# Layer-norm scaling of layers one and two moved from VectorE to ScalarE, with an offset computed on GpSimd, in a four-layer graph network kernel

## The reference

```python
x = _layernorm(x + L0(x, nodemask, adj, adj, ...))   # attention, 8 heads, mixed with adj and exp(-adj)
x = _layernorm(x + L1(x, adj, W))                    # relu([x, adj@x/deg] @ W.T)
x = _layernorm(x + L2(x, adj, ...))                  # two hypergraph convolutions, relu and layer norm between
x = _layernorm(x + L3(x, adj, ...))                  # gated attention over adj

def _layernorm(x, axis=-1, eps=1e-05):
    m = jnp.mean(x, axis=axis, keepdims=True)
    v = jnp.var(x, axis=axis, keepdims=True)
    return (x - m) / jnp.sqrt(v + eps)
```

## Time and profile before

| what | value |
|---|---|
| median of 3 runs | 1185.15 us |
| the profiled execution | 1184.85 us, span 1182.8 us |
| mean granted TensorE clock | 0.986 of full |
| PE busy | 1127.0 us (95%) |
| DVE busy | 919.8 us (78%) |
| ACT busy | 595.7 us (50%) |
| POOL busy | 572.5 us (48%) |

### The profile page before, as it was taken

How to read it: one execution, slowest core, us unless ns; L and a number is a source line. 1 busy time by engine, 2 the same in 40 slices (tenths; PEclk the granted TensorE clock), 3 DMA queues, 4 the chain that set the end, 5 groups by cost and what they waited for, 6 DMA issues and landing times.

```text
span 1182.8 us, 29171 instructions
## 1 busy us (share of the span) xinstructions
PE 1127.0 (95%) x10416; PEld 951.4 (80%) x10416; DVE 919.8 (78%) x2223; ACT 595.7 (50%) x1266; POOL 572.5 (48%) x731
## 2 busy tenths in 40 slices
PE   5889999999999999999999999999999999999875
PEld 4768888888888888888888888888888888888763
DVE  6675887878788887878877788788778878777865
ACT  2536465454646445474544647454464645546331
POOL 2426356382644628264472735537273553826341
PEclk9899999999999999999999999999999999999897
DMA  7010102010010201001020100102001010100000
GB/s 233 24 28 1 46 3 67 1 48 21 22 44 0 67 0 44 22 22 44 0 67 0 43 24 22 44 0 67 0 23 44 18 49 0 42 8 28 2 23 18
DMA packets 52868, 37.22 MB, mean 31 GB/s; under 512 B 28182, under 2 KB 47707, under 8 KB 52827
## 3 DMA queue, kind: packets, MB, share of 16 engines
q1 hardware_dynamic: 51272, 35.09, 9.7%
q10 hardware_dynamic: 1554, 1.58, 0.5%
HBM read 28.27 MB, written 8.39 MB: 31 GB/s over the span
## 4 chain that ended last, share of the span: by engine, by line
PE 90%; DVE 5%; ACT 2%; POOL 1%; issue 1%; DMA 0%; SPq 0%; POOLq 0%; DVEq 0%; ACTq 0%
PE bank L1022 22%; PE bank L1024 21%; PE bank L1023 20%; PE bank L1093 3%; PE bank L1128 3%; PE bank L1163 2%; PE bank L1220 2%; PE bank L1201 2%; PE bank L1106 2%; PE bank L1294 2%; PE bank L1258 2%; DVE oT_lo L709 2%; PE bank L1083 1%; PE bank L1284 1%; PE bank L1248 1%; PE bank L1182 1%
## 5 line engine op out<-in xcount | busy, mean ns | idle before, releaser
L529 POOL TENSOR_TENSOR prob<-prob,srec 128x512 f32<-128x512 f32 x64 | 71.6, 1118 | 146.9 <-DVE srec L832 146.9
L467 POOL TENSOR_SCALAR var<-mv 128x2 f32<-128x2 f32 x128 | 29.0, 227 | 208.6 <-DVE mv L779 208.6
L786 DVE TENSOR_SCALAR x<-x,mv,rstd 128x256 f32<-128x256 f32 x256 | 119.0, 522 | 3.8 <-POOL rstd L470 3.3
L590 ACT ACTIVATE v<-bank 64x256 f32<-64x256 f32 x256 | 96.7, 378 | 17.7 <-PE bank L1024 15.4
L477 POOL TENSOR_TENSOR bhT<-hT,be 128x512 f32<-128x512 f32 x16 | 18.3, 1144 | 168.3 <-PE bank L1172 168.3
L775 DVE BATCH_NORM_STATS2 stats<-x 128x6 f32<-128x256 f32 x256 | 96.4, 418 | 4.4
L470 POOL TENSOR_TENSOR rstd<-var,negh 128x2 f32<-128x2 f32 x128 | 91.1, 712 | 10.7
L534 POOL TENSOR_TENSOR prob<-prob,mix 128x512 f32<-128x512 f32 x64 | 86.7, 1355 | 6.0 <-POOL prob L529 1.9
L918 DVE TENSOR_TENSOR hT_lo<-r,hT_hi 128x512 fp32r<-128x512 f32 x64 | 69.7, 1089 | 22.4 <-ACT hT_hi L633 22.2
L1022 PE MATMUL bank<-wo_hi,oT_hi 128*128 128x256 f32 x256 | 75.1, 293 | 8.9 <-DVE oT_lo L709 8.9
L1022 PE MATMUL bank<-w_hi,hT_hi 128*128 128x258 f32 x256 | 75.8, 296 | 2.7 <-DVE hT_lo L918 2.1
(11 more groups left out here) (202 smaller groups left out, 3697.9 us busy)
## 6 DMA issues: line engine op xcount, KB each, us to landing
xTin<-in_x_t SPq DMA_DIRECT2D x32, 256.0 KB, 2.8
xin<-in_x SPq DMA_DIRECT2D x16, 512.0 KB, 3.7
out_x<-x SPq DMA_DIRECT2D x32, 256.0 KB
adjA<-in_adj SPq DMA_DIRECT2D x16, 128.0 KB, 2.5
adjB<-in_adj_t SPq DMA_DIRECT2D x32, 64.0 KB, 3.1
adjC<-in_adj_t SPq DMA_DIRECT2D x32, 64.0 KB, 2.3
r<-in_wqkv ACTq DMA_DIRECT2D x2, 512.0 KB, 4.1
x<-in_wqkv SPq DMA_DIRECT2D x1, 512.0 KB, 8.2
```

What stands on the lines that cost most here:

```text
L529: pool.tensor_tensor(rows_of(u), rows_of(u), srec[:, k, :].rearrange("p (h a) -> p h a", a=1) .broadcast_to([P, 2 * HP, N]), ALU.mult).the ...
L590: ins = act.activation(v[e * N:(e + 1) * N, i, gr, :, :], src[gr * N:(gr + 1) * N, e], ACT.Copy)
L786: ins = dve.tensor_scalar(x[:, t, :], x[:, t, :], mv[layer][:, t, 0:1], rstd[layer][:, t:t + 1], ALU.subtract, ALU.mult)
```

## The change

The steps `scale0` and `scale1` go from VectorE's order to ScalarE's. ScalarE computes x * rstd + offset with one activation (Identity, per-partition scale and bias) for each tile. GpSimd makes the offset: after `rstd` it multiplies the mean by `rstd` in place and multiplies that by -1 into `var`, with a wait on its own semaphore before each. Layers 2 and 3 keep VectorE's `scale`.

```diff
+SHIFTED = (0, 1)
 ACT_ORDER = [
 ...
-    ("A", "v", 0), ("D", "y3", 3), ("B", "graph_d", 0), ("A", "shift", 1), ("A", "v", 1), ("B", "spread", 0),
+    ("D", "y3", 2), ("A", "v", 0), ("D", "y3", 3), ("B", "graph_d", 0), ("A", "shift", 1), ("A", "v", 1),
+    ("B", "scale1", 0), ("B", "spread", 0), ("B", "spread", 1), ("A", "v", 2), ("B", "up", 0), ("B", "hid_hi", 0),
 ...
-    ("N", "k", 0), ("N", "q", 0), ("N", "q", 1), ("B", "hyper", 0), ("N", "q", 2), ("B", "hyper", 1), ("N", "q", 3),
+    ("A", "pv", 2), ("A", "pv", 3), ("N", "k", 0), ("N", "q", 0), ("N", "q", 1), ("B", "hyper", 0),
+    ("A", "scale0", 0), ("N", "q", 2), ("B", "hyper", 1), ("N", "q", 3), ("A", "scale0", 1),
 ]
@@ inv_root, on GpSimd
                 pool.tensor_tensor(rstd[layer][:, lo:hi], var[layer][:, lo:hi], negh[:, lo:hi],
                                    ALU.pow).then_inc(SEM[f"rstd{n}"], 1)
+                if layer in SHIFTED:
+                    pool.wait_ge(*count(f"rstd{n}", g, k + 1))
+                    apart(pool, g)
+                    pool.tensor_tensor(mv[layer][:, lo:hi, 0], mv[layer][:, lo:hi, 0], rstd[layer][:, lo:hi],
+                                       ALU.mult).then_inc(SEM[f"mean_rstd{n}"], 1)
+                    pool.wait_ge(*count(f"mean_rstd{n}", g, k + 1))
+                    apart(pool, g)
+                    pool.tensor_scalar(var[layer][:, lo:hi], mv[layer][:, lo:hi, 0], -1.0, None,
+                                       ALU.mult).then_inc(SEM[f"offset{n}"], 1)
@@ on ScalarE
+            def scale(g, layer, x, lo, hi, ready, k):
+
+                act.wait_ge(*count(f"offset{layer}", g, k + 1))
+                for t in range(lo, hi):
+                    ins = act.activation(x[:, t, :], x[:, t, :], ACT.Identity, bias=var[layer][:, t:t + 1],
+                                         scale=rstd[layer][:, t:t + 1])
+                ins.then_inc(SEM[ready], 1)
 ...
+                "scale0": lambda g, i: scale(g, 0, xl[0], 2 * i, 2 * i + 2, "x1_ready", i),
+                "scale1": lambda g, i: [scale(g, 1, xl[1], 2 * k, 2 * k + 2, "x2_ready", k) for k in range(2)],
@@ on VectorE
             def scale0(g, i):
-                scale(g, 0, xl[0], 2 * i, 2 * i + 2, "x1_ready", i)
                 if isinstance(g, int) and g == 0 and i == 1:
                     other_weights(3)
 ...
-                "scale1": lambda g, i: [scale(g, 1, xl[1], 2 * k, 2 * k + 2, "x2_ready", k) for k in range(2)],
```

More of the change, by code:

```diff
@@ L116 @@
 PER = {
-    "xT_in": 32, "x_in": 16, "adjA_in": 16, "adjB_in": 32, "adjC_in": 32, "mask_in": 16, "out_done": 32, "xT_hi": 2, "xT_lo": 2, "mask_rows": 2,
+    "xT_in": 32, "x_in": 16, "mean_rstd0": 2, "offset0": 2, "mean_rstd1": 2, "offset1": 2, "adjA_in": 16, "adjB_in": 32, "adjC_in": 32, "mask_in": 16, "out_done": 32, "xT_hi": 2, "xT_lo": 2, "mask_rows": 2,
     "xb_ready": 1, "expA_ready": 1, "mix_sum": 1, "mix_ready": 1,
```

## The result

The changed kernel takes 1251.05 us (median of 4 runs, 1250.60 to 1252.28) against 1185.01 us before: a ratio of 1.056, 95% interval 1.054 to 1.058. It is slower, as forecast, but by 66 us where 43 were forecast, and 1251.05 lies above the range of 1212 to 1246. The profiled span is 1249.6 us against 1182.8.

The account below looks back on a forecast made before the run. TensorE was taken as the bound, busy 69.35 of 69.79 us a round. The terms 35 + 3.5 + 0.8 + 6.3 + 0.9 - 3.1 = 43.4 us on 1184.85 gave 1228 us, range 1212 to 1246.

Parts of the forecast that it names:

- `spread`, 14 groups: Groups 1 to 14: layer 1's scalings queue behind `v 1`, making TensorE's tile 2 2.5 us late: 35 us (30 to 36).
- `spread`, group 0: Group 0, where ScalarE is behind with `v 1`: the last layer 1 scaling ends 3.5 us late.
- `spread`, group 15: Group 15, which has no `v`: scalings 1.35 us late, of which a later wait takes back some 0.5: 0.8 us.
- `turn1`, 14 groups: End of the round: layer 0's second scaling pair makes `turn1`'s tile 2 0.45 us late: 6.3 us (1.5 to 8.5).
- group 15's open chain: Group 15, where PE waits 3.56 us for the scaling: GpSimd's two operations and ScalarE's pair add 0.9 us.
- `mask` of group 0: Group 0: PE's 3.3 us wait for `mask` falls to 1.4 and the clock stays up: gain 3.1 us (1.9 to 3.6).
- The upper ends: ScalarE's price: the second per-partition operand costs as much as the first, 0.59 us a scaling, 0.49 from start to start.
- Identity needed no other table: Rival on ScalarE: Identity isn't in the loaded table, costing 5.1 us in each of 15 rounds: 1305 us; chance 0.02.
- Hidden, as forecast: GpSimd's added 2.8 us a round fits beside 34 us of idle time, with nothing on the path.
- the clock falls in every round: Rival: behind `spread`'s pause TensorE runs at 1.2 GHz, 16 times, adding 19 to 27 us: 1247 to 1255; chance 0.13.
- in a few rounds only: Milder form of the clock rival: some rounds lose the clock, adding 2 to 8 us, which the range holds.
- the two tiles inside the pause: Argument against the clock rival: `spread`'s 2.4 us pause is in two pieces, with two tiles of work inside.

Follow-up runs that it names:

- E: The changed kernel with layer 1's scaling moved earlier in ScalarE's order, behind `y3 0` instead of `v 1`: 1188.97 us, ratio 1.004.
- F: The changed kernel with 7 unread 128x512 products before tile 0 of `spread` (14 in group 0, none in group 15): 1233.66 us, ratio 1.041.
- the split one: The changed kernel with layer 0's scaling back on VectorE, only layer 1's on ScalarE: 1237.34 us, ratio 1.045.

## Why the forecast was wrong, step by step

The account of the 66.8 us between the spans, from differences of periods: before, changed, the kernel with layer 1 early (E, whose full rounds are 70.32 us, its first 61.51 and its 15th 64.34), and the one with `spread` filled (F: 73.03, 64.87 and 67.03).

| step | forecast | measured | from |
|---|---|---|---|
| `spread`, 14 groups | 35 | 37.9 | 14 x (73.03 - 70.32) |
| `spread`, group 0 | 3.5 | 3.4 | first period, F - E |
| `spread`, group 15 | 0.8 | 0.6 | `turn1`'s x6 row to `up`: 28.38 - 27.77 |
| `turn1`, 14 groups | 6.3 | 7.4 | 14 x (70.32 - 69.79) |
| group 15's open chain | 0.9 | 0.9 | 64.34 - 62.52 - 0.53 = 1.3, less 0.4 inside `turn1` |
| `mask` of group 0 | -3.1 | -3.1 | first period, E - before |
| sum | 43.4 | 47.1 | |
| clock, 10 rounds | 0 | 15.8 | 10 x 1.58 |
| clock, group 0 | 0 | 1.2 | first period, changed - F |
| before the first `turn1` | 0 | 1.5 | 66.78 - 65.27 |
| the last 50 us (put down to the clock, not shown) | 0 | 1.2 | 52.98 - 51.82 from `up` to the end |

Together 66.8. Every mechanism in the sum was right, and its 47.1 us alone would have stayed inside the range; two sizes were a little small (2.71 us for 2.5, 0.53 for 0.45), and with the clock up the kernel would be where the filled one is, 1233.66 us, inside the range.

*ScalarE's price.* The upper ends, 0.59 us and 0.49 from start to start, were right: 590 ns, and 2.07 us for four against 2.06. The Trainium skill (ScalarE: Activation LUTs, "What ACT_TABLE_LOAD costs") gave 0.585; the trace agrees, so the second per-partition operand costs as much as the first. Identity needed no other table.

*GpSimd.* Hidden, as forecast, and shown by the run that added only its work.

*`mask` in group 0.* The wait fell to 0.8 us and not to 1.4, because TensorE comes later out of `turn1`, where it now waits itself. From the start of `turn1` to the product that needs `mask`, TensorE takes 3.85 us in the kernel with layer 1 early against 5.73 before: 1.9 us less, as forecast. The clock stays at 1.00 behind it, which is the rest of the 3.1.

*Group 15.* The parts were priced well in sum, not in kind. Its waits, of TensorE and then of ScalarE, against the earlier trace rows:

```profile
1164.69 0.41 PE L1182 MATMUL bank<-ident,x 128*128 128x128 f32 x2 [1.14 <-ACT x L641]
1168.24 1.54 PE L1182 MATMUL bank<-ident,x 128*128 128x128 f32 x6 [3.14 <-ACT x L641]
```

```profile
1162.93 0.63 ACT L668 ACTIVATE r<-r 128x512 f32<-128x512 f32 x1 [3.63 <-POOL r L525]
1163.47 1.08 ACT L641 ACTIVATE x<-x,var,rstd 128x256 f32<-128x256 f32 x2
```

The first pair stands behind a tanh that waited 3.63 us for GpSimd. I had looked at the second pair only.

*The step that failed* is the weighing of the clock. In the sum it had no term at all. The forecast put "the clock falls in every round" at 0.13 and "in a few rounds only" at 2 to 8 us. It was neither: 10 of 13, 17.0 us. The rival's price was right (up to 1.7 us a time, 1.6 measured); its chance was not. That 1251.05 lies inside the rival's 1247 to 1255 is partly luck: it had 16 losses, on a sum that was 3.7 us too small. The argument against it leaned on one pause of 1.7 us that had kept the clock and on the two tiles inside the pause. One pause that kept it says little, since pauses of 1.98 and 0.21 us both kept it and lost it in this one kernel. The two tiles did not protect either: the pause in one piece of 2.32 us lost 5 of 13 rounds, the split one 5 of 13 in a round of nearly the same length. What those rows could carry was "some rounds, number unknown", 0 to 16 times 1.6 us, a range of 1228 to 1254 with no reason to favour its low end.

*The start.* The 1.5 us ahead of the first `turn1` aren't charged to the change: in runs where nothing ahead of it was changed it came at 65.27 to 67.89 us. In the last 50 us the kernel before runs at half clock in part too, so their 1.2 us aren't charged to the change either; one stretch of before and then one of after, each beginning 25.0 us behind the first product of `up`:

```profile
1155.98:1165.98 10.00, 8.56 (x35) 6.33 (x36) 3.59 (x8) 2.75 (x5) 0.00 (x0) 0.63 0.00 0
```

```profile
1221.62:1231.62 10.00, 8.37 (x23) 6.33 (x24) 3.36 (x7) 2.55 (x4) 0.00 (x0) 0.51 0.00 0
```

## What to carry to other kernels

An engine with half its time free is not free where the work is put: ask what stands ahead of the new step in that engine's order, and when the consumer asks. Here the same four activations cost 38 us and the clock behind `v 1`, and nothing where the last of them ends 8.6 us before `spread` asks (496.89 against 505.50 in the kernel with both layers early). And when a change opens a pause of about 2 us on a TensorE that is otherwise dense, price the clock with the pause. Here it was about 1.6 us each time it fell, in a number of rounds that the trace of the kernel before couldn't give, so the range should have held none and all of them.

## What the runs showed of the hardware

- Two pauses of 1.98 and 0.21 us, with 0.68 us of work between them, are followed by 1.00 in some rounds of one execution and by about 3 us at 0.50 in others.
- How many rounds lose it changed with the length of the round. With the pause unchanged, 0.5 us more work took 5 of 13 to 9 (one run each traced). By the Trainium skill (TensorE: Matmul & The Clock Gate, "Part 1: The HAM clock gate") the chip watches TensorE's activity on a clock of its own, which does not start over with the kernel. The regular order of lost rounds agrees with that; no run here looks at that clock itself.
- 1.97 us of work that nobody reads, put into the pause of each round, made the kernel 17.4 us faster (1251.05 to 1233.66): no full round lost the clock.
- The activation of 128x256 with two per-partition operands takes 590 ns, and 0.49 us from start to start.
